# A 3x3 convolution with pairs of output columns from four transformed products instead of six

## The reference

```python
def _gn(v, G=32, eps=1e-5):            # group norm of 8 channels over the whole image
    ...
    return ((g - m) / jnp.sqrt(s + eps)).reshape(v.shape)

# _L0_conv_ref(_gn(x), ...): NH = 8 heads, DK = DV = 64, 192 convolution outputs
conv_out = lax.conv_general_dilated(x, conv_w, (1, 1), 'SAME', ('NHWC', 'HWIO', 'NHWC')) + conv_b   # 3x3, 256 -> 192
kqv = jnp.einsum('bhwc,co->bhwo', x, qkv_w) + qkv_b                                                  # 1x1, 256 -> 192
k, q, v = kqv[..., :DK], kqv[..., DK:2 * DK] * DKH ** (-0.5), kqv[..., 2 * DK:]
logits = q k^T + rel_w + rel_h          # relative logits: q against 63 keys of each axis
attn = softmax(logits) v                # 8 images x 8 heads x 1024 x 1024
...
x = x + concatenate([conv_out, attn @ attn_w + attn_b])
# layer 1: self attention over 1024 tokens, then a routed feed-forward (2 of 8 experts), layer norm
```

## Time and profile before

| what | value |
|---|---|
| median of the timed runs | 2333.66 us |
| the profiled execution, its device time | 2336.84 us |
| its span | 2334.7 us |
| TensorE busy | 2169.2 us, 93% of the span |
| VectorE busy | 1338.4 us, 57% |
| ScalarE busy | 1234.2 us, 53% |
| mean granted TensorE clock | 0.954 of full speed |

### The profile page before, as it was taken

The page is one execution under the profiler, slowest core; times in us unless marked ns, Lnnn a source line. Parts: engine busy times, 40 slices in busy tenths (PEclk is TensorE's granted clock), DMA queues, the critical chain, the costliest instruction groups (busy, mean ns, idle before and its releaser), DMA issues. The chain is left out here.

```text
span 2334.7 us, 28195 instructions
## 1 busy us (share of the span) xinstructions
PE 2169.2 (93%) x10536; PEld 1480.5 (63%) x10536; DVE 1338.4 (57%) x1977; ACT 1234.2 (53%) x2160; POOL 248.4 (11%) x260
## 2 busy tenths in 40 slices
PE   4999999988999999999999983799999987999997
PEld 3777888875445445454554521677777775888886
DVE  6223333427777777777777702466666653655565
ACT  1212222321577777777777771566666654656564
POOL 1000000001111122121122200000000000000000
PEclk7999999985899999999999995999999997999999
DMA  2232353368767777666777204233333115354331
GB/s 76 80 91 69 97 183 122 134 195 211 134 108 110 111 111 119 109 110 116 107 110 117 88 10 126 89 109 107 106 108 107 47 46 212 132 186 177 137 136 54
DMA packets 144951, 268.35 MB, mean 115 GB/s; under 512 B 24368, under 2 KB 88624, under 8 KB 140848
## 3 DMA queue, kind: packets, MB, share of 16 engines
q1 hardware_dynamic: 135696, 240.67, 42.7%
q0 software_dynamic: 7680, 25.17, 3.3%
q10 hardware_dynamic: 1440, 0.71, 0.1%
HBM read 156.60 MB, written 107.24 MB: 113 GB/s over the span
## 5 line engine op out<-in xcount | busy, mean ns | idle before, releaser
L677 DVE TENSOR_REDUCE a_nmax<-a_sm 128x1 f32<-128x1024 f32 x512 | 602.9, 1219 | 176.7 <-PE a_sm L697 176.7
L928 ACT ACTIVATE p_shared<-a_st 128x512 f32<-128x512 f32 x1024 | 556.9, 597 | 235.6 <-PE a_st L953 234.1
L968 PE MATMUL a_pv<-p_shared,a_va 128*32 128x512 f32 x2048 | 272.5, 604 | 0.9 <-ACT p_shared L928 0.9
L953 PE MATMUL a_st<-a_qf,a_kf 121*128 121x512 f32 x704 | 254.4, 439 | 10.2 <-ACT p_shared L928 8.0
L953 PEld LDWEIGHTS a_st<-a_qf,a_kf 121*128 121x128 f32 x704 | 119.2, 189 | 208.5 <-ACT p_shared L928 198.0
L697 PE MATMUL a_sm<-a_kf,a_qf 120*128 120x512 f32 x704 | 217.5, 431 | 6.7 <-DVE a_nmax L677 3.7
L1817 PE MATMUL x_h_ps<-x_v_hi,x_w 128*128 128x512 f32 x512 | 184.1, 401 | 0.0
L1831 PE MATMUL x_y_ps<-x_h_hi,x_w 128*128 128x512 f32 x512 | 180.7, 394 | 0.0
L1727 DVE SCALAR_TENSOR_TENSOR x_h_lo<-x_hid,x_wts,x_h_hi 128x512 fp32r<-128x512 f32 x128 | 95.9, 750 | 139.3 <-ACT x_h_hi L1688 139.2
L697 PEld LDWEIGHTS a_sm<-a_kf,a_qf 120*128 120x128 f32 x704 | 135.3, 202 | 57.9 <-DVE a_nmax L677 23.9
L1684 ACT ACTIVATE x_hid<-x_h_ps,x_bias 128x512 f32<-128x512 f32 x128 | 88.4, 691 | 140.5 <-PE x_h_ps L1817 140.5
(11 more groups left out here) (259 smaller groups left out, 3536.6 us busy)
## 6 DMA issues: line engine op xcount, KB each, us to landing
x_w<-w_d SPq DMA_DIRECT2D x31, 1024.0 KB, 8.9
rel_d<-p_shared SPq DMA_DIRECT2D x12, 2048.0 KB, 13.1
a_qf<-rel_d SPq DMA_DIRECT2D x22, 512.0 KB
a_qf<-rel_d SPq DMA_DIRECT2D x44, 256.0 KB
c_x_st<-in_x SPq DMA_DIRECT2D x8, 1024.0 KB, 7.0
va_d<-c_va SPq DMA_DIRECT2D x16, 512.0 KB, 4.7
a_va<-va_d SPq DMA_DIRECT2D x32, 256.0 KB, 23.8
a_w_st<-in_L_ffn_W POOLq DMA_DIRECT2D x32, 256.0 KB, 7.1
```

What stands on the lines that cost most here:

```text
L677: nc.vector.tensor_reduce(nmax[:, h, t:t + 1], sm[k % 2][:], axis=AX.X, op=ALU.max, negate=True).then_inc(sm_read, 1)
L928: nc.scalar.activation(probs[:, t % 2, h, half * HALF:(half + 1) * HALF], st[half][:], ACT.Exp).then_inc(exp_done, 1)
L953: nc.tensor.matmul(st[half][:], kf[j][0:ROW_M + 1, h, t * P:(t + 1) * P], qf[j][0:ROW_M + 1, h, 2 * t // TT, half * HALF:(half + 1) * HALF ...
L968: m = nc.tensor.matmul(pv[32 * h:32 * h + 32, cols], va[j][:, t, h, :], probs[:, t % 2, h, cols], start=t == 0, stop=t == TT - 1, skip_gro ...
```

## The change

The convolution along a row is transformed. For each pair of output columns (2n, 2n+1) and the four inputs d0..d3 that they need, four transformed inputs are made: v0 = d0 - d2, v1 = d1 + d2, v2 = d2 - d1, v3 = d1 - d3, each as an image of 34 x 16 in high and low parts. The three taps (g0, g1, g2) of a row become g0, (g0+g2)+g1, (g0+g2)-g1 and g2, with factors of one half applied to the products 1 and 2 afterwards. The even output is m0 + (m1+m2)/2, the odd one (m1-m2)/2 - m3. A unit is now `("c0", t)` or `("c1", t)` with t = 0 to 3 for the product, over all 32 rows and 16 pairs (again 512 columns). The projections kq and v need the centre pixel alone: even pixels are (v1 - v2)/2, odd ones (v1 + v2)/2. Two more things move: rel set 4 loses its own staging and set 0 begins in image 3; and the first attention block makes its set 1 before its set 0.

```diff
+        u_st = staging[:, ...].rearrange("p (u k a o) -> p u k a o", u=2, k=KC, a=3)
+        factor = (by_column[:, 0], u_st[:, 0], u_st[:, 1], by_column[:, 2])
+        w0_hi = sb("c_w0_hi", [P, 4, KC, 3, P], f32r)
...
-        y_even = sb("c_y_even", [P, 2, KC, HP, WP], f32r)
-        y_odd = sb("c_y_odd", [P, 2, KC, HP, WP], f32r)
+        y = sb("c_y", [P, KC, H, WP])
+        v = [sb(f"c_v{i}", [P, 2, KC, HP, PAIRS], f32r) for i in range(SLOTS)]
+        v32 = sb("c_v32", [P, KC, H, PAIRS])
...
-        UNITS = [("kq", 0), ("conv0", 0), ("kq", 1), ("conv0", 1), ("v", 0), ("conv1", 0), ("v", 1), ("conv1", 1)]
+        UNITS = [("kq", 1), ("kq", 2), ("v", 1), ("v", 2), ("c0", 1), ("c0", 2), ("c1", 1), ("c1", 2),
+                 ("c0", 0), ("c1", 0), ("c0", 3), ("c1", 3)]
...
+        ORDER = [UNITS] * (FIRST - 1) + [
+            with_rel(0, (("c1", 1), 2), (("c1", 2), 2), (("c0", 0), 2), (("c1", 0), 2)),
...
+            UNITS[:5] + rel(4, 0, 4) + UNITS[5:6] + rel(4, 4, 8) + UNITS[6:11] + rel(5, 0, 4) + UNITS[11:] + rel(5, 4, 8)]
...
 SyncE, image(b):
+                    sp.wait_ge(mix_ready, b + 1)
+                    sp.dma_start(mixT_d[b, 0], cst[:, 0, :]).then_inc(cst_stored, 16)
...
+                    if b == B - 1:
+                        store_relative(b, RELS_OF[b][1])
...
 ScalarE:
+                def normalize(p):
+                    act.wait_ge(rstd_ready, p + 1)
+                    for c in range(KC):
+                        rows = y[:, c, :, 1:W + 1]
+                        last = nc.scalar.activation(rows, rows, ACT.Identity, bias=shift[:, c:c + 1], scale=rstd[:, c:c + 1])
+                    last.then_inc(y_ready, 1)
+                def round_v(p, u):
...
+                    nc.scalar.activation(inner(s[:, 0]), v32[:], ACT.Copy).then_inc(vhi_ready, 1)
...
 VectorE:
+                def make(p, u):
+                    dve.wait_ge(y_ready, p + 1)
+                    if nth(p, u):
+                        dve.wait_ge(v_ready, nth(p, u))
+                    a, b, op = ((0, 2, ALU.subtract), (1, 2, ALU.add), (2, 1, ALU.subtract), (1, 3, ALU.subtract))[u]
+                    cols = lambda o: y[:, :, :, o:o + W - 1:2]
+                    nc.vector.tensor_tensor(v32[:], cols(a), cols(b), op).then_inc(v_made, 1)
+                def low_v(p, u):
+                    nc.vector.tensor_tensor(inner(s[:, 1]), v32[:], inner(bits(s[:, 0])), ALU.subtract).then_inc(v_ready, 1)
...
+                                nc.vector.scalar_tensor_tensor(even, acc[n][:], 0.5, first[:], ALU.mult, ALU.add)
+                                nc.vector.scalar_tensor_tensor(odd, acc[n][:], -0.5, first[:], ALU.mult, ALU.add).then_inc(unit_read[n], 1)
+                            if t == 0:
+                                nc.vector.tensor_tensor(even, even, acc[n][:], ALU.add).then_inc(unit_read[n], 1)
+                            if t == 3:
+                                nc.vector.tensor_tensor(odd, odd, acc[n][:], ALU.subtract).then_inc(unit_read[n], 1)
...
+                for b in range(B):
+                    image(b, b + 1 < B)
+                    if b == 0:
+                        relative_keys()
...
 TensorE:
+                    rows = range(3) if what in ("c0", "c1") else (1,)
+                    i, total = 0, KC * len(rows) * (2 if what in ("v", "c1") else 3)
...
+                                m = nc.tensor.matmul(acc[n][:].rearrange("p (y x) -> p y x", x=PAIRS), wt, vp[:, k, dy:dy + H, :],
+                                                     start=i == 0, stop=i == total - 1)
...
 first attention block, ScalarE:
-                act.wait_ge(first_stored, 32 * 5)
-                for r, (wh, g) in enumerate(RELS):
+                for i, r in enumerate(TURNS):          # TURNS = (1, 0)
+                    if r == 0:
+                        act.wait_ge(first_stored, 32 * 6)
 ... and SyncE:
-                    sp.wait_ge(rel_lo, RU * (r + 1))
+                    sp.wait_ge(rel_lo, RU * (TURNS.index(r) + 1))
```

More of the change, by code:

```diff
@@ L192, in _, with store_relative @@
                 sp.sem_inc(va_stored, 16 * GROUPS)
+                def store_relative(b, r):
+                    n = r * RU + RU - 1
+                    sp.wait_ge(unit_read[bank(b, "rel", n)], read(b, "rel", n))
+                    wh, g, images = r % 2, r // 2 % 2, slice(0, FIRST) if r < 4 else slice(FIRST, B)
+                    for part in range(2):
+                        sp.dma_start(rel_d[images, g, wh, part].rearrange("b p n -> p b n"), bits(hl[:, part])).then_inc(rel_stored, 16)
                 def image(b, ahead):
@@ L532, in image, with turn_values @@
-                def image(b, s, prefetch):
-                    pe.wait_ge(y_ready, b * KC + KC)
-                    for what, t in units(b):
-                        unit(b, s, what, t)
-                        if prefetch and (what, t) == ("kq", 0):
-                            turn(b + 1)
-                        if prefetch and (what, t) == ("conv0", 0):
-                            group_mean(b + 1)
-                        if prefetch and (what, t) == ("conv0", 1):
-                            group_dev(b + 1)
-                    pe.wait_ge(unit_read[bank(b, "v", 1)], read(b, "v", 1))
+                def turn_values(b, prefetch):
+                    pe.wait_ge(unit_read[bank(b, "v", 2)], read(b, "v", 2))
@@ new lines, in image @@
+                def image(b, prefetch):
+                    for what, t in units(b):
+                        unit(b, what, t)
+                        if prefetch and (what, t) == ("kq", 2):
+                            turn(b + 1)
+                        if prefetch and (what, t) == ("c0", 1):
+                            group_mean(b + 1)
+                        if prefetch and (what, t) == ("c0", 2):
+                            group_dev(b + 1)
+                        if (what, t) == ("c1", 2):
+                            turn_values(b, prefetch)
@@ L554, in _ @@
                 pe.wait_ge(consts, 2)
-                turn(0, first=True)
+                turn(0)
                 group_mean(0)
                 group_dev(0)
-                all_images(pe, image)
+                pe.wait_ge(consts, 4)
+                for b in range(B):
+                    image(b, b + 1 < B)
 def attention(nc, q_all, bd_hi, bd_lo, shared, first_stored, kq_d, rel_d, va_d, att_d, w1, w2, w_d, b1, b2, bias_d):
@@ L723, in attention @@
         BANKS = 4
-        rels = [("rel", r, n) for r in range(len(RELS)) for n in range(RU)]
+        TURNS = (1, 0)
+        rels = [("rel", i, n) for i in range(len(RELS)) for n in range(RU)]
         passes = [("logits", 0, t) for t in range(AHEAD)] + [("pass", s, None) for s in range(STEPS)]
```

529 lines of the change are left out of this document (295 added, 234 removed).

## The result

| | before | after |
|---|---|---|
| median of the runs, us | 2334.05 (4 runs, 2333.65 to 2341.8) | 2220.07 (4 runs, 2214.51 to 2221.66) |
| ratio | | 0.95, 95% interval 0.9473 to 0.9526 |
| profiled execution, span | 2334.7 | 2216.8 |

The changed kernel is 5% faster; forecast was 2222 in 2206 to 2262. The median is right to 2 us, but several terms of the sum were not, and they happened to cancel in large part. (The profiled execution took 2218.53 us, and the forecast for it was 2224.6.) First the stretches of the changed kernel, cut at the first kq product of each image (23.74 is image 0's, 69.38 image 1's), at TensorE's last conv-phase instruction (378.15), at the first rel product of the attention block (382.06), at its first `a_sm` product (424.53) and at its first `a_st` product (474.80). The columns are those of the earlier trace rows.

What follows compares the result with a forecast made beforehand. TensorE was taken to bound the convolution phase. Terms -117.3 - 12.4 + 3.0 + 4.7 + 5 - 0.7 + 5.5 = -112.2 us gave 2224.6 us profiled, 2222 median, range 2206 to 2262.

Steps and rivals of the forecast that it cites:

- Products removed: Convolution phase: 140 instead of 200 TensorE products per image, over eight images at 0.2444 us each; -117.3 us.
- Pace: Remaining 1120 convolution products: unbroken operands run at 0.2333 instead of 0.2444 us each; -12.4 us, bounds 0 and -12.4.
- rival B: Convolution products stay at 0.2444 us because weight loading, not broken rows, sets the pace; +12.4 us, about 2235; chance 0.14.
- Start: Before image 0's first products: work begins behind the weights, there at 24.98 us; -1.6 us.
- Image 0: First image: TensorE waits for VectorE's transforms and weight splits, partly at low clock; 43.2 us long, +6.6 - 2.0.
- Key tables: Image 1: kq evictions and statistics queue behind the key tables on VectorE, so TensorE waits; +4.7 us, bounds 0 and 6.8.
- Rel images: Images with rel units: image 5 waits about 1 us, image 7 about 3, others near nothing; +5 us, bounds 1 and 15.
- VectorE can follow: Convolution phase: VectorE needs 26.7 of 36.6 us per plain image; next kq's needs met with 7 us in hand.
- Rival A: Convolution phase: VectorE becomes the bound through accesses to every second float32; +40 us, about 2262; chance 0.18.
- Border: Between convolution phase and attention: four rel units run behind the last c1 unit, covering last addition and store; -0.7 us.
- First attention block: Set 5's 4 MB store delays the first query loads, so the maxima begin about 5 us late; +5.5 us, bounds 0 and 14.
- Rival C: Convolution phase: new waits bring TensorE's granted clock down, 31 us more per plain image; 2340 and more; chance 0.04.

Runs made afterwards that it cites:

- run 9: Changed kernel with the 12 products of every c1 unit made twice into the same sums (384 more products); 2303.83 us.
- run 12: Changed kernel with high and low rows of each transformed input laid out alternately and the whole tile moved by 16 B; 2218.71 us.
- run 11: Changed kernel with high and low rows of each transformed input laid out alternately, so a product reads 32 rows of 16 numbers with gaps; 2229.27 us.
- run 1: Changed kernel with the values' bias loaded wide as before the change, once for each of 8 token tiles; 2227.8 us.
- run 2: Kernel before the change, with only the small load of the values' bias (128 x 64 numbers); 2319.28 us.
- run 3: Changed kernel with the 16 key-table instructions cut into two pieces of 8, placed in VectorE's waits of images 0 and 1; 2214.59 us.
- run 4: Changed kernel with set 0's 8 rel products in image 3 placed two each behind c0_1, c0_2, c1_1, c1_2; 2216.32 us.
- run 10: Changed kernel with every low part of a transformed input subtracted twice on VectorE; 2253.77 us.
- run 6: Changed kernel with set 5's rel products in image 7 moved four behind c1_0 and four behind c0_3; 2225.32 us.
- run 5: Changed kernel with set 5's 4 MB store issued behind the first attention block's query and key loads; 2232.02 us.
- run 7: Changed kernel with key tables, set 0 and set 5 products moved, and set 5's store issued ahead of the mixT stores; 2208.63 us, ratio 0.9449.

## Why the prediction was right, and which of its terms were wrong

**Products removed, -117.3: right.** The rows of a plain image (52.83 to 36.44) and run 9 show it. **Pace, -12.4: the number right, its reason wrong, and so luck.** 0.2325 was measured for a forecast of 0.2333, but "the row breaks are the only difference that I see" named the wrong difference; by run 12 a broken operand is as quick. On run 11's placement 9 of rival B's 12 us came back (1.13 an image), and nothing in the earlier trace rows could tell.

**Start, -1.6: mis-sized, it was -13.1.** The step "weights are there at 24.98" took over from the earlier trace rows a time that the diff itself removes: that row names the load of `c_vb` as what ended the wait, and the diff makes that load an eighth. Runs 1 and 2 put it at 10.0 to 10.5 us. It is the largest error of the sum; the line is in the full diff, though not in the excerpt above.

**Image 0, 43.2 us: it took 45.64.** Beyond VectorE's queue there was one I hadn't played: ScalarE was still rounding weights, behind a transform of VectorE for which it had stood 3.0 us, when the first kq sum was ready, and TensorE waited 3.4 us for its bank.

**Key tables, +4.7: mechanism right, mis-sized, +6.4.** The wait was 3.9 us at the place forecast; the low clock behind it, 2.5 us, was left out. Run 3 takes both away.

**Rel images, +5: the sum near, the places wrong.** Over five plain images the images 3 to 7 take 47.25 us, where the images 4 to 7 before took 41.9 over four plain ones: +5.35. But forecast were waits in images 5 and 7. Images 5 and 6 had 0.55 each over image 4, image 7 had 0.2 us of waits, and image 3 had 5.0, by the place of its products behind c1_1 (run 4). Again about half was the clock (2.2 of 5.0).

**VectorE can follow: true for the changed kernel, with less in hand than I said.** "Met with 7 us in hand" is contradicted by run 10: of about 5 us added in that place a plain image took up some 2.5, and the rel images nearly nothing on the mean. Rival A's mechanism was absent, but A's price (+40) is about what 5 us of VectorE an image cost there (+34): the ground on which it stood was closer than its chance of 0.18, given for the stride alone, made it look.

**Border, -0.7: it was -3.75,** by the rel units that cover the last addition; run 6, without that cover, has 7.84 us again.

**First attention block, +5.5: mechanism right, mis-sized, +9.9.** In the changed kernel's DMA windows (382 to 390, 390 to 398, 398 to 410):

```profile
382.00:390.00 8.00, 7.06 (x32) 6.90 (x32) 2.53 (x4) 2.39 (x4) 5.27 (x8) 0.50 1.02 402
390.00:398.00 8.00, 7.21 (x34) 7.21 (x34) 4.61 (x8) 1.87 (x4) 0.00 (x0) 0.50 1.08 236
398.00:410.00 12.00, 12.00 (x58) 12.00 (x58) 7.11 (x7) 6.83 (x8) 0.00 (x0) 0.50 0.97 68
```

The store moves at 400 GB/s and is through in 10 us, not the 16 forecast. It left 1.9 us ahead of the block and not 5. (The prediction's own figures, 16 us of which 5 go ahead, leave 11 behind the border, not its 13.) The loads behind it, 8 to 32 partitions wide, keep the engines just as busy at 68 GB/s. The first `a_sm` products, before and then after:

```profile
543.13 1.19 PE L697 MATMUL a_sm<-a_kf,a_qf 120*128 120x512 f32 x2 [3.03 <-issue]
```

```profile
424.53 2.05 PE L811 MATMUL a_sm<-a_kf,a_qf 120*128 120x512 f32 x4 [12.99 <-DMA a_kf<-kq_d]
```

I took the query copy for the last thing that `a_sm` waits for, and gave it 4 us. It starts at +28.3, sooner than my +34, but the keys land 14.2 us behind its start. The old kernel had `a_sm` 12.2 us behind the copy's start too, and the copy takes 3.60. TensorE idled its last 3.03 us there, and of the semaphores for which the code waits only the loads' was left, so the loads' tail set that block already; it stood out 3 us past the rel products, and no slack was there to hide the store's 10 us. Runs 5, 6 and 7 move the 10 us about and never lose them. How the 14.2 us divide is open: the next 4 MB store was issued at 413.88 and ran beside the keys' last bytes. The Trainium skill (SBUF — State Buffer, Door 1: The DMA port swizzle) says that a transfer's rate goes by how many of the 16 SBUF ports its partitions reach; 16 neighbouring partitions reach four. A quarter of the 435 GB/s that it gives for all ports is an estimate of 109, and half of that, 54, for the 8 partitions of a kq or key load. The trace has 68 in the narrow stretch, where by the order of issue loads of both kinds run, and 400 in the wide one: the rule fits as far as these windows can tell.

**Rival C: its mechanism occurs, at a tenth of its price.** The waits of images 1 and 3 brought a lower clock, with 2 to 3 us of loss each time, and it came back to 1.00 by itself. At the border the 3.9 us pause has the same effect, and with waits behind it the clock stays at 0.50 through the first attention block, as before.

In sum, of the differences from the forecast, start (-11.5) and border (-3.05) against the phase (+3.8: image 0 2.5, key tables 1.7, rel images 0.4, less 0.8 by the plain ones), the block (+4.4) and what follows (+0.7) leave -5.7 for the profiled span. Of this the medians show 2, since the profiled execution lay 3.2 above its median before and 1.5 below it after. The total was hit in part by luck.

## What to carry to other kernels

Go through a diff for the small loads too: a row named the transfer that ended the wait at the start, and the one line that changed it brought 10 of 114 us. When products get fewer, look at which chains on the other engines lose their cover, and test the slack by adding work to the engine instead of counting its idle time, bearing in mind in which chain the added work stands; moving 24 small instructions and 8 products into places with cover gave 11 us more. A large store ahead of narrow loads cost its own length here, and each of the three orders tried moved that to another wait; earlier data or fewer bytes were not tried.

## What the runs showed of the hardware

- The pace of a 512-column fp32r product, weights changed each time, was 0.2308 to 0.2444 us: 0.2325 unbroken, 0.241 in rows of 16 numbers with gaps, 0.2308 for the same rows 16 B further on, and 0.2444 in the rows of 32 with gaps before the change. The cause is open.
- Pauses of TensorE of 3.9 us in one piece (image 1) and of 2.8 us in two (image 3) were followed by a lower granted clock (0.50 and 0.58 in the next 4 us) and cost 2.5 and 2.2 us on top of themselves; in runs 3, 6 and 12 image 3's cost 3.6 to 3.9.
- Narrow loads held the DMA engines at a busy share of 0.97 while moving 68 GB/s (398 to 410 us), and a 4 MB store moved 402 GB/s at 1.02; share and rate must be read together.
- Behind the first `a_st` product the same instructions took 1736.3 to 1745.5 us from kernel to kernel, so that a single total can't settle a question of 5 us.
